# Attention kernel: one run and one value section for each key tile on the diagonal, rows of maxima ahead of the next quad's loads, and the next quad's first tiles beside the last steps

## What is computed

```python
def reference(x, Wq, Wk, Wv, Wo, weight, bias, gamma, beta):   # x: (2, 2048, 512), all float32
    xn = layernorm(x)
    q, k, v = (xn @ W for W in (Wq, Wk, Wv))          # 16 heads of 32
    scores = einsum('bthd,bshd->bhts', q, k) * tril(ones((T, T)))   # masked scores are 0, not -inf
    attn = softmax(scores / T ** 0.5)
    s = einsum('bhts,bshd->bthd', attn, v) @ Wo
    g = silu(layernorm(xn, gamma, beta) @ ternary(weight).T + bias)
    return x + s * g
```

## Time and profile before

| | |
|---|---|
| time, median of 3 runs | 1579.03 us (1577.02 to 1579.18) |
| time of the profiled execution | 1579.03 us |
| its span, first to last instruction | 1577.3 us |
| PE / DVE / POOL / ACT busy | 1497.4 / 1053.3 / 870.8 / 773.8 us |
| instructions | 24547 |
| mean granted TensorE clock | 0.984 |

### The profile page before, as it was taken

How to read it: one execution, slowest core, us unless ns; L and a number is a source line. 1 busy time by engine, 2 the same in 40 slices (tenths; PEclk the granted TensorE clock), 3 DMA queues, 4 the chain that set the end, 5 groups by cost and what they waited for, 6 DMA issues and landing times.

```text
span 1577.3 us, 24547 instructions
## 1 busy us (share of the span) xinstructions
PE 1497.4 (95%) x8554; PEld 905.5 (57%) x8554; DVE 1053.3 (67%) x2389; ACT 773.8 (49%) x1614; POOL 870.8 (55%) x723
## 2 busy tenths in 40 slices
PE   6999999999979999999999999999999999998876
PEld 5788888887434455454554555545545455544755
DVE  7545755643857777777777777777777777752566
ACT  4333322233545566655666555665665655665110
POOL 4100000000655877878778777787776877679341
PEclk9999999999889999999999999999999999999988
DMA  6668866549830460252155146045016311212998
GB/s 213 182 179 229 245 199 181 168 144 229 199 85 25 92 148 22 66 127 65 36 114 122 36 87 149 17 92 139 25 48 127 97 36 38 95 39 79 315 340 279
DMA packets 110426, 201.42 MB, mean 128 GB/s; under 512 B 14688, under 2 KB 32736, under 8 KB 109280
## 3 DMA queue, kind: packets, MB, share of 16 engines
q1 hardware_dynamic: 99216, 177.86, 42.5%
q10 hardware_dynamic: 11088, 22.02, 4.4%
HBM read 123.22 MB, written 76.28 MB: 126 GB/s over the span
## 4 chain that ended last, share of the span: by engine, by line
PE 76%; DMA 10%; DVE 7%; SPq 2%; ACT 2%; issue 1%; POOL 1%; ACTq 1%; POOLq 0%; DVEq 0%
PE psP L1288 20%; PE psS L1366 17%; PE psM L1266 15%; PE psO L1389 15%; PE psL L1395 5%; DMA half<-mrow 5%; DMA gr<-gate 4%; DVE mx L1077 2%; DVE psM L1074 2%; PE psL L1404 2%; PE psT L1213 2%; ACT Pb L937 1%; SPq L576 1%; SPq L673 1%; DVE oo L1201 1%
## 5 line engine op out<-in xcount | busy, mean ns | idle before, releaser
L814 POOL TENSOR_TENSOR acc<-acc,Pb 128x1024 f32<-128x1024 f32 (+2 forms) x308 | 600.1, 1978 | 175.0 <-PE psO L1389 143.9
L937 ACT ACTIVATE Pb<-psS 128x512 f32<-128x512 f32 (+2 forms) x1122 | 516.4, 533 | 292.2 <-PE psS L1366 286.3
L1077 DVE TENSOR_REDUCE mx<-psM 128x1 f32<-128x512 f32 x768 | 484.5, 683 | 163.4 <-PE psM L1266 161.8
L1366 PE MATMUL psS<-half 97*128 97x512 f32 (+1 forms) x1247 | 472.1, 397 | 22.0 <-DMA half<-mrow 17.5
L1266 PE MATMUL psM<-half 96*128 96x512 f32 (+3 forms) x1280 | 457.1, 385 | 7.7 <-DVE mx L1074 4.6
L1366 PEld LDWEIGHTS psS<-half 97*128 97x128 f32 x1247 | 234.7, 190 | 254.9 <-issue 96.9
L1074 DVE CUSTOM_DVE_ANT_0 psM<-psM,negm 128x256 f32<-128x256 f32 (+3 forms) x512 | 237.6, 518 | 81.4 <-PE psM L1266 81.4
L1266 PEld LDWEIGHTS psM<-half 96*128 96x128 f32 x1280 | 236.1, 191 | 85.0 <-DVE mx L1077 28.3
L1389 PE MATMUL psO<-Pb,Vs 128*32 128x512 f32 (+3 forms) x2304 | 267.6, 535 | 2.4 <-POOL Pb L797 2.4
L797 POOL TENSOR_SCALAR_AFFINE_SELECT Pb<-Pb 128x256 f32<-128x256 f32 x240 | 94.1, 408 | 83.2 <-ACT Pb L937 80.1
L937 ACT ACTIVATE acc<-psS 128x512 f32<-128x512 f32 x125 | 65.9, 601 | 123.5 <-PE psS L1366 123.2
(11 more groups left out here) (101 smaller groups left out, 1461.5 us busy)
## 6 DMA issues: line engine op xcount, KB each, us to landing
half<-q_hi SPq DMA_DIRECT2D x32, 512.0 KB, 12.8
half<-k_hi SPq DMA_DIRECT2D x32, 512.0 KB, 10.6
xt<-in_L_attn_x SPq DMA_DIRECT2D x8, 1024.0 KB, 7.9
q_hi<-st_hi SPq DMA_DIRECT2D x32, 256.0 KB, 4.4
q_lo<-st_lo SPq DMA_DIRECT2D x32, 256.0 KB, 4.8
gate<-gs SPq DMA_DIRECT2D x32, 256.0 KB, 2.2
k_hi<-st_hi SPq DMA_DIRECT2D x32, 256.0 KB, 2.8
k_lo<-st_lo SPq DMA_DIRECT2D x32, 256.0 KB, 2.9
```

The lines of the kernel that those rows point to most:

```text
L814: g.tensor_tensor(to[:, :, o:], to[:, :, o:], Pb[s % RING][:, heads, o:], ALU.add).then_inc(sum_done, 1)
L937: a.activation(weights(s, h)[:, o:], score_bank(s * HQ + h, last)[:, o:], ACT.Exp, scale=SCALE).then_inc(exp_done, 1)
L1077: ins = v.tensor_reduce(flat[:, heads, slots], bank[:, 0:ns * w].rearrange("p (a b c) -> p a b c", a=nh, c=w), AX.X, ALU.max)
L1366: t.matmul(score_bank(n, last)[:, o:], Ks[par][j // HALF][0:MROW + 1, h, j % HALF * P:(j % HALF + 1) * P], Qs[par][c // 2][0:MROW + 1, h, ...
```

## The change

On the diagonal the order becomes that of the other groups: R(s+2) V(s) R(s+3) V(s+1). Step 38's share of maxima goes with step 0 of the next quad, step 39's with its step 1; step 1 is run by itself only in quad 0. ACT covers the shares of steps 38 and 39 too. In SP's order the loads of the next quad's upper halves and values move behind `store_maxima(qn, 2)` and `load_chunk(qn, 2)`, and quad 0 issues them there for quad 1, so that only a lower half and the rows of ones remain ahead of quad 0.

```diff
@@ SP, ahead of the quads
-            for half in range(2):
-                load_half(1, 1, half)
-                load_ones(1, half)
-            load_values(1, 1)
+            load_half(1, 1, 0)
+            load_ones(1, 0)
+            load_ones(1, 1)
@@ SP, quad
                     load_chunk(qn, 1)
-                    if more:
-                        sp.wait_ge(pv_done, START + qn * NSTEP)
-                        load_half(qn + 1, 1 - par, 1)
-                        load_values(qn + 1, 1 - par)
                 store_chunk(qn, 0)
                 store_maxima(qn, 2)
                 load_chunk(qn, 2)
+                if more:
+                    sp.wait_ge(pv_done, START + qn * NSTEP)
+                    load_half(qn + 1, 1 - par, 1)
+                    load_values(qn + 1, 1 - par)
@@ ACT, exps
-                    if s >= 2:
-                        max_rows(max_share(qn, s - 2, h))
+                    max_rows(max_share(qn, s - 2, h) if s >= 2 else max_share(qn - 1, NSTEP + s - 2, h))
@@ PE, quad
-                run(1, (qn, par), None)
                 if qn == 0:
+                    run(1, (qn, par), None)
                     pe.wait_ge(cs_done, START + NCHUNK * NQ)
                 def ahead(s):
                     if s + 2 < NSTEP:
                         run(s + 2, (qn, par), s)
-                    elif s + 2 > NSTEP and more:
-                        run(0, (qn + 1, 1 - par), s)
+                    elif more:
+                        run(s + 2 - NSTEP, (qn + 1, 1 - par), s)
                     else:
                         run(None, None, s)
 
                 for gr, (c, j) in enumerate(GROUPS):
                     s = 2 * gr
                     ahead(s)
-                    if on_diagonal(s):
-                        ahead(s + 1)
                     values(s)
                     if j == 0 and (c > 0 or follows):
                         row_sums(*((qn, c - 1, not more) if c else (qn - 1, NCH - 1, False)))
-                    if not on_diagonal(s):
-                        ahead(s + 1)
+                    ahead(s + 1)
                     values(s + 1)
```

## The result

The kernel after the change takes **1563.63 us**, median of 4 runs (1562.62 to 1565.81), against 1578.03 for the kernel before beside it: a ratio of 0.991, 95% interval 0.9893 to 0.9928. In a second set of runs it was 0.9892 (0.9869 to 0.9915). The profiled execution took 1562.81 us, with a span of 1561.1, 16.2 less than before. Forecast were 1555 us, a gain of 24 against one of 14 to 16.

The account below looks back on a forecast made before the run. PE's order was taken to bound the attention, its waits coming second. The terms 11.2 + 0 - 1.1 + 2.4 + 0.7 - 0.6 + 11.5 = 24.1 us, off 1579.03, gave 1555 us; range 1546 to 1569.

Parts of the forecast that it names:

- (D): Across quads, counted holds of PE are taken up by waits left in elsewhere: 7.2 us, time 1548 us; chance 0.12.
- (B): Only quad 0 gains; POOL and ACT hold PE at boundaries, quads come out even: 1568.5 us; chance 0.2.
- (A): The forecast itself, PE's order setting the attention's time: 1555 us, own range 1549 to 1562; chance 0.6.
- Rows of maxima, quad 0: Quad 0, R10 to V11: fewer loads queued ahead end PE's 9.5 us wait; a gain of 11.5 us.
- Chunk 1, quads 1 to 6: R10 to V11: the wait for rows of maxima goes, but V8 waits 1.3 us for POOL's select; gain 0.
- The second hold: Chunk 1: R11, its select and POOL's adds come late, so exponentials of step 13 wait, another 0.4 us.
- Boundaries: R38 to V3 of the next quad: from 21.98 to 20.4 us, 1.6 at each of seven, 11.2 us.
- Chunk 2: R22 to V23: POOL's selects are early, so a gain of 0.3 us in each of eight quads, 2.4 us.
- Start of quad 0: First four steps of quad 0: gain 0.7 us, as DVE gets the value sections to catch up.
- Quad 7: Loss of 1.1 us in chunk 1, where nothing waits for the rows, and 0.6 at the end, behind POOL.
- The price of a change of kind: Wherever PE alternates one run and one section: 0.33 us extra, 64 more on the diagonal, 21 us.
- (C): V(s) waits for its select on every diagonal group: 36 us more, 1591 us; chance 0.08.

Follow-up runs that it names:

- e3_masked_late: The whole change, with POOL's masked keys of chunk 1 moved behind the selects of steps 8 and 9: 1555.63 us, 0.985 of the kernel before.
- e4_first_tiles: The whole change, but the diagonal keeps its old order R(s+2) R(s+3) V(s) V(s+1): 1554.82 us, 0.9848 of the kernel before.
- f2_start_old: The whole change, but steps 0 to 3 of quad 0 in the old order: 1559.6 us, 0.9883 of the kernel before.
- e6_pairs: `e4_first_tiles` with the order R(s+2) R(s+3) V(s) V(s+1) off the diagonal too, quads 1 to 7: 1583.41 us, 1.0032 of the kernel before.
- f3_loads_again: The kernel before with only SP's load order of the change, run once more: 1564.41 us, 0.9912 of the kernel before.

## Why the prediction was right, and where its sizes were off

The time lies in the range from (D) to (B) and the direction is right; it lies 1.6 us outside (A)'s own range, 1549 to 1562. The gain was overestimated by 8 us in the profiled execution and 10 in the median, and part of that is chance: spells fell on the stretches that I compared, and 1.7 us of the profile's gain lie outside the attention. The mechanisms held, several terms did not. By its steps:

- **Rows of maxima, quad 0: forecast 11.5, measured 11.1 on the stretch that was forecast (R10 to V11, 24.2 to 13.1), and 11.6 in the second trace of the whole change (to 12.65).** The cause was the queue, as said, and the size too. From V7 to V12 the gain is 9.8 in the first trace, 11.0 in the second and 10.9 with SP's part alone; the 1.2 us between the first two are the clock, at half from 430.4 to 433.8, over V7 and R10. I had not counted on a spell in a stretch without a wait. V12 to V19 gains 1.6 because a spell at 484.5 did not come this time; in the second trace of the whole change this stretch took 34.9 again. Such spells are worth 1 to 2 us each and don't belong to the change.
- **Chunk 1, quads 1 to 6: forecast 0, measured a loss of 0.12 each.** V8's wait is there, with the size given (R10 and V8 together 1.3 us over). The profile lists 0.66 of it as idle time of PE. The second hold, 0.4 for the exponentials of step 13, did not come in the kernel after (R13 takes 1.96 us, an ordinary 1.9); it came with SP's part alone, where nothing ahead of it was late. What came in its place I had left out: R11, four narrow scores and two maxima, takes 1.32 us for 0.76 of matmuls, as it did before (1.28). Its fourth score starts 0.05 us after the exponential of its first one ends. `e3_masked_late` settles the cause.
- **Boundaries: forecast 1.6 each, measured 1.05.** This is the step that was mis-sized in every quad: the eight runs were taken as matmuls and changes of kind, with 0.45 us of waits in all. I priced a change of kind at 0.33 us, from runs of 384 and 512 columns. The eight value sections of a boundary are indeed 0.14 over their matmuls each, 1.1 us together; but the eight runs take 12.93 us for 10.39 of matmuls, 0.32 each instead of 0.19, and the excess is largest in R3, R1 and R2 (0.4 to 0.5), which are narrow. At the boundary behind quad 0, in each of these three, the fourth score starts 0.05 us after the exponential of the first one has ended and its bank is free, so ACT holds them, one exponential at a time. The 0.45 that I had are part of that. `e4_first_tiles` shows that 0.84 of the 1.05 has nothing to do with the diagonal's order.
- **Chunk 2: forecast 0.3, measured 0.3** in seven quads. In quad 7, which has no maxima there, the new order loses 0.4 with its two more changes of kind: 0.2 each, with no wait to set against them.
- **Start of quad 0: forecast a gain of 0.7, measured a loss of 1.5** (2.7 in the comparison side by side). I reckoned with DVE's waits and not with the clock. That the order of steps 0 to 3 does it is shown by `f2_start_old` in the trace, and the four traces compared there put nearly all of it down to the longer spell.
- **Quad 7: forecast losses of 1.1 and 0.6, measured 1.5 in chunk 1, and 2.3 from V24 on.** The second is in part a spell of 6.8 us from 1427.1 on; in the second trace it is 1.1. It is not measured closely: with the old order from V24 on this stretch takes 39.6 to 41.0 us in seven traces, with the new one 40.7 to 43.2 in five.
- **The price of a change of kind against the rule of the Trainium skill.** That rule of the Trainium skill ("TensorE: Matmul & The Clock Gate", Part 3: weight loads are pulled ahead of matmuls in flight) would have made the sum 20 us better still if it held at each change of kind. It is further from what was measured than the row that I went by, and quad 7's chunk 2 and the group at 582.31 show a price.

Against the rivals: (B), only quad 0 gains, is refuted at the boundaries, though its time, 1568.5, is nearer to the measured one than mine. (C), a wait for the select at every diagonal group, did not happen: PE's wait for POOL's selects stands in the trace eight times, at V8 of quads 1 to 7 and V36 of quad 7. What I had not set up as a rival is the one that matters: that the two halves of the change are worth very different amounts. SP's part gives all of the gain, 0.991; PE's and ACT's part gives 0.9998; and inside that second part the first tiles win what the new order on the diagonal loses.

## What to carry to other kernels

A wait that shows only 1 to 2 us in each pass may hide the next one: taking it away at chunk 1 gave 0.7 us of 1.3, because POOL's add was due next. Alternating runs and sections pays where the runs outpace the banks behind them (full widths with many maxima) and costs 0.2 to 0.3 us each time where they do not, so decide it by place and not by one rule for all groups. Before changing the order on one engine, count what a measured stretch holds in both orders: in `e6_pairs` two stretches got shorter in a kernel that was slower. And before putting a consumer earlier, look up when the engine that feeds it starts that piece of work: here moving 3 us of POOL's work behind the selects of two steps was worth 1.1 us a quad in the new order and nothing in the old.

## What the runs showed of the hardware that was not expected

The granted clock falls to half for spells of 3.4 us inside long stretches where PE never stands still for more than a fraction of a microsecond (430.4 in the kernel after; 549.9, 809.3, 939.1 and 1198.5 with SP's part alone), and at such a place once for 6.8 us (431.7 in `e3_masked_late`) and once for 10.2 (427.1 in `f3_loads_again`), at different places in two executions of one kernel. Each of those of 3.4 us costs 1.1 to 1.7 us, about as much as a whole boundary gains, the two long ones 2.1 and 3.0. So single profiles of these kernels differ by a few us from one to the next.
